# One product of the maxima moved ahead of the two scores in TensorE's order

## What is computed

```python
q = rope(h @ w_down_q.T @ w_up_q.T)          # 16 heads of 64
k = rope(h @ w_down_kv.T @ w_up_k.T)
v = h @ w_down_kv.T @ w_up_v.T
scores = einsum('bhqd,bhkd->bhqk', q, k) / 8
attn = softmax(scores, axis=-1)
out = einsum('bhqk,bhkd->bhqd', attn, v) @ w_out.T + residual
```

## Time and profile before

| | |
|---|---|
| runs: median, lowest, highest | 4357.19, 4356.98, 4368.64 us |
| profiled execution: own time | 4368.48 us |
| profiled execution: span, mean granted TensorE clock | 4366.7 us, 0.967 |
| TensorE matmul busy | 4005.4 us, 92% |
| GpSimd busy | 3049.4 us, 70% |
| ScalarE busy | 3010.3 us, 69% |
| VectorE busy | 2756.6 us, 63% |
| first and last S | start at 613.2 and 3799.9 us of the span |

### The profile page before, as it was taken

How to read it: one execution, slowest core, us unless ns; L and a number is a source line. 1 busy time by engine, 2 the same in 40 slices (tenths; PEclk the granted TensorE clock), 3 DMA queues, 4 the chain that set the end, 5 groups by cost and what they waited for, 6 DMA issues and landing times. The chain is left out here.

```text
span 4366.7 us, 65862 instructions
## 1 busy us (share of the span) xinstructions
PE 4005.4 (92%) x24896; PEld 2256.7 (52%) x24896; DVE 2756.6 (63%) x3555; ACT 3010.3 (69%) x3800; POOL 3049.4 (70%) x1597
## 2 busy tenths in 40 slices
PE   7999869999899989999998999899889999879999
PEld 6888724444344434444444444344444444358888
DVE  5556457656766675766667666766776667345653
ACT  4454348787778777877887787788777887735444
POOL 3444438878778787878887788788877887724444
PEclk9999979999999999999999999999999999979999
DMA  3333221111111211121112112111211121123332
GB/s 109 100 117 107 79 77 52 50 57 61 62 57 54 69 50 57 55 78 53 50 60 69 52 62 69 49 50 59 71 52 59 50 79 52 41 92 117 117 100 66
DMA packets 193645, 301.12 MB, mean 69 GB/s; under 512 B 50766, under 2 KB 101680, under 8 KB 192688
## 3 DMA queue, kind: packets, MB, share of 16 engines
q1 hardware_dynamic: 193328, 296.92, 21.2%
HBM read 201.92 MB, written 26.74 MB: 52 GB/s over the span
## 5 line engine op out<-in xcount | busy, mean ns | idle before, releaser
L988 DVE TENSOR_REDUCE atNM<-atPS 128x2 f32<-128x1024 f32 x1024 | 1205.9, 1220 | 804.0 <-PE atPS L806 801.4
L1053 POOL TENSOR_TENSOR atACC<-atACC,atPT 128x1024 f32<-128x1024 f32 x512 | 1285.1, 2510 | 63.0 <-ACT atPT L922 10.3
L922 ACT ACTIVATE atPT<-atPS 128x1024 f32<-128x1024 f32 x1024 | 995.7, 1023 | 201.7 <-PE atPS L827 195.1
L913 ACT ACTIVATE atPS<-atSH 128x1024 f32<-128x1024 f32 x1024 | 1009.5, 1022 | 87.1 <-DVE atNM L988 45.0
L838 PE MATMUL atPO<-atPT,atV 128*64 128x512 f32 x4096 | 974.3, 596 | 0.0
L1053 POOL TENSOR_TENSOR atACC<-atPT 128x1024 f32<-128x1024 f32 x256 | 624.0, 2437 | 105.3 <-PE atOT L849 103.7
L1032 POOL TENSOR_TENSOR atVT<-atVT,atSIN 128x512 f32<-128x512 f32 x256 | 342.8, 1339 | 366.6 <-DMA atVT<-atR 366.5
L806 PE MATMUL atPS<-atKH,atQH 64*128 64x512 f32 x2048 | 465.1, 455 | 121.0 <-ACT atPT L922 95.1
L838 PEld LDWEIGHTS atPO<-atPT,atV 128*64 128x64 f32 x4096 | 281.2, 137 | 477.1 <-issue 470.4
L827 PE MATMUL atPS<-atQH,atKL 64*128 64x512 f32 x2048 | 476.9, 462 | 45.2 <-ACT atPS L913 45.2
L827 PE MATMUL atPS<-atQH,atKH 64*128 64x512 f32 x2048 | 413.4, 399 | 0.0
(11 more groups left out here) (238 smaller groups left out, 6593.2 us busy)
## 6 DMA issues: line engine op xcount, KB each, us to landing
atVT<-atR SPq DMA_DIRECT2D x512, 128.0 KB, 2.0
atSH<-atMD SPq DMA_DIRECT2D x128, 512.0 KB, 4.4
f1GB<-f1GD SPq DMA_DIRECT2D x128, 256.0 KB, 6.8
atRSUM<-atRD SPq DMA_DIRECT2D x128, 256.0 KB, 4.0
f2GB<-f2GD SPq DMA_DIRECT2D x128, 256.0 KB, 6.9
x<-X SPq DMA_DIRECT2D x7, 1024.0 KB, 4.8
X<-x SPq DMA_DIRECT2D x7, 1024.0 KB, 5.4
f1XB<-in_x SPq DMA_DIRECT2D x5, 1024.0 KB, 5.3
```

What stands on the lines that cost most here:

```text
L913: act.eng.activation(PS[ring.of[("score", n, t, j)]][:, :, :], SH[t][:, :, :], ACT.Copy).then_inc(filled[j % 2].sem)
L922: act.eng.activation(PT[k % NPT][:, :, :], PS[ring.of[step]][:, :, :], ACT.Exp, scale=SCALE).then_inc(grown.sem)
L988: dve.eng.tensor_reduce(NM[:, q // 4, :, q % 4, t], PS[ring.of[step]][:, :, :], AX.X, ALU.max, negate=True).then_inc(most_out.sem)
L1053: pool.eng.tensor_tensor(total[:, :, :], begun[:, :, :], PT[k % NPT][:, :, :], ALU.add).then_inc(gathered.sem)
```

## The change

On each period's place in `order`, M0 now stands ahead of S0 and S1, and M1 stays behind them. No instruction is added or taken away.

```diff
@@ -671,7 +671,7 @@
-                order += begin.get(g, []) + scores + mosts + early.get(g, []) + fills + attends
+                order += begin.get(g, []) + mosts[:1] + scores + mosts[1:] + early.get(g, []) + fills + attends
```

## The result

The changed kernel takes 4515.8 us (median of four runs, 4505.5 to 4530.6), the kernel before 4362.9 beside it: the ratio is 1.035, with a 95% interval from 1.032 to 1.038. It is slower by some 153 us. 101 were forecast: the time lies inside the stated range, which reached to 4545, but 13 us above the forecast's own bounds of 4413 to 4503.

The account below looks back on a forecast made before the run. The prediction took TensorE, busy 92% of the span, as the bound. Its terms gave +13.5 us per sequence, 7 x 13.5 + 6.5 = 101 in all, so 4458 us against a median of 4357.2; range 4350 to 4545.

Parts of the forecast that it names:

- The mechanism: Turn of the ring: M1 no longer waits for E0 but for X0, so VectorE's lateness at X0 delays TensorE.
- some 250 us: Sign in the table of waits: M's wait for X, replacing its 95 us wait for an exponential.
- periods with VectorE free: 28 periods of a sequence: M1 at 1.82 instead of 2.08 us, -0.26 each, -7.3 us per sequence.
- periods 0 and 1 of the even pairs: In period 1, M0 and the scores behind it wait for the queries' copy: +1.2 us each, +4.8 per sequence.
- period 5 of pairs 1, 5, 7: VectorE is busy until 1.82 us into the period, so M1 comes late: +1.0 each, +3.0 us per sequence.
- period 5 of pairs 0 and 6: A rotation of 2.62 us runs into the period and delays X0: +1.5 each, +3.0 us per sequence.
- three more periods of a sequence: Three periods into which a rotation of up to 2.9 us or `qlow` runs: 1.0 each, +3.0 us per sequence.
- norm pairs 2 and 3, periods 4 to 6: VectorE is behind with the layer norm: +1.4 us for each of five periods, +7.0 per sequence.
- Rival 1: VectorE begins X0 earlier and late rotations no longer reach into the next period: 4322 us, chance 0.13.
- Rival 2: Rotations stay pinned to GpSimd's gathers, some six periods of a sequence lose 0.7 us each: 4492 us, chance 0.16.
- Rival 3: Nothing is absorbed: norm-pair periods pay M1's full delay, 5 us in about four periods: 4556 us, chance 0.10.
- rival 4: It evens out: blocked periods cost half, gains and losses cancel: 4357 us, chance 0.08.

## Why the prediction was right, and what it sized too small

*The mechanism* was right: M1 waits for X0, and with the table of tiles, which keeps TensorE's order and takes that wait away, the periods that were long by a late X0 are gone. The sign of "some 250 us" of M waiting for X came with 245. The size is another matter. The parts of the sum, in us over all eight sequences, and what the two traces show from S0 to S0:

| part | forecast | measured |
|---|---|---|
| periods with VectorE free (206 that are in no other row) | -58 | -54 |
| periods 0 and 1 of the even pairs | +38 | +55 |
| period 5 of pairs 1, 5, 7 | +24 | +23 |
| period 5 of pairs 0 and 6 | +24 | +43 |
| three more periods of a sequence | +24 | +9 |
| period 6 of pairs 1, 5, 7 | none | +22 |
| norm pairs 2 and 3, periods 4 to 6 | +49 | +38 |
| periods 0 and 1 of pair 3 | none | +19 |
| period 7 of pair 1 | none | -14 |
| all others | none | +11 |
| sum | +101 | +152 |

Some parts came out dearer than forecast, by about 90 us together, and others cheaper, by about 40. That the total is no further off than 51 is in part luck.

*Free periods.* The -0.26 us a period is right: 212 at -0.263 came.

*Period 5 of the odd pairs.* +1.0 was forecast, +0.91 is the median.

*Period 1 of the even pairs.* The step was right and the term too small: +1.2 each, 38 us, against 55 in the trace of the change and 46 in the experiment that takes it out. M0 comes 7.6 us after period 0 begins, as worked out. In pair 32 the two periods lose 2.4 even so, and the clock is why. The copy, M0 behind it and the first products of S0:

```profile
2297.12 1.05 ACT L896 ACTIVATE atQH<-atU 128x1024 fp32r<-128x1024 f32 x1
...
2298.32 0.79 PE L806 MATMUL atPS<-atKH,atQH 64*128 64x512 f32 x2 [3.38 <-ACT atQH L896]
2298.88 0.65 PE L827 MATMUL atPS<-atQH,atKL 64*128 64x512 f32 x2
...
2299.31 0.65 PE L827 MATMUL atPS<-atQL,atKH 64*128 64x512 f32 x2
```

TensorE has stood still for 3.38 us, and the products then follow every 0.43 us instead of 0.23. In pair 48 it stands still for as long, the products keep their pace, E0 starts 1.4 us behind the copy as forecast, and the two periods lose 1.25:

```profile
3142.41 0.50 PE L806 MATMUL atPS<-atKH,atQH 64*128 64x512 f32 x2 [3.37 <-ACT atQH L896]
3142.72 0.43 PE L827 MATMUL atPS<-atQH,atKL 64*128 64x512 f32 x2
3142.95 0.42 PE L827 MATMUL atPS<-atQL,atKH 64*128 64x512 f32 x2
...
3143.64 1.94 ACT L922 ACTIVATE atPT<-atPS 128x1024 f32<-128x1024 f32 x2 [1.38 <-PE atPS L827]
```

The windows (span, busy of five engines, granted clock, DMA) of period 1 of pair 32 and of pair 36, which loses 1.5 after a shorter wait of 2.07:

```profile
2298.30:2305.00 6.70, 6.68 (x45) 4.36 (x47) 3.58 (x3) 4.20 (x5) 6.56 (x3) 0.78 0.00 0
...
2517.30:2522.50 5.20, 5.20 (x43) 3.02 (x42) 4.35 (x3) 4.03 (x5) 3.96 (x3) 1.00 0.00 0
```

The granted clock averages 0.78 in the one, part of it at the lower of its two levels, and 1.00 in the other. So it goes in all pairs 0 and 4. In seven of them the clock is 1.00 in the 3 us from M0 on, and they lose 1.2 to 1.6 us, from S0 to S0. In the other nine it is 0.50 to 0.72 there, and they lose 2.4 to 3.8. The kernel before has 1.00 at this place in all of them but the very first. The forecast priced the wait, not what may come to the clock behind it.

*Period 5 of pairs 0 and 6.* +1.5 was forecast, the median is +3.4. The step "a rotation of 2.62 runs into the period" did not come: the rotation now starts ahead of the gather and ends 0.57 into the period. It is the inverse (L997) behind it that falls beside the gather, and takes 2.34 us. X0 begins at 3.07, where 2.3 to 2.7 was forecast. Pair 32:

```profile
2320.57 2.82 POOL L1053 TENSOR_TENSOR atACC<-atPT 128x1024 f32<-128x1024 f32 x1
...
2321.07 2.34 DVE L997 TENSOR_TENSOR atRQ<-atRQ 128x16 f32<-128x16 f32 x1
...
2324.93 0.61 PE L806 MATMUL atPS<-atKH,atQH 64*128 64x512 f32 x2 [2.46 <-DVE atNM L988]
2325.47 1.97 PE L785 MATMUL atOT<-atCQ,atWQ 128*64 128x512 f32 x4
```

The projection takes 1.97 instead of 1.08 behind it: the clock again. In pair 38 it stays at 1.00 behind the same wait, and the period loses 1.8:

```profile
2646.73 0.50 PE L806 MATMUL atPS<-atKH,atQH 64*128 64x512 f32 x2 [2.46 <-DVE atNM L988]
2647.17 1.08 PE L785 MATMUL atOT<-atCQ,atWQ 128*64 128x512 f32 x4
```

Four periods with such a wait keep the clock and lose 1.8 each; ten have 0.50 to 0.75 in the 3 us behind M1 and lose 3.4 to 3.7. In the two places together the lower clock is worth some 28 us (an estimate: ten times 1.65, and eight times 1.4 in the pairs 0 and 4), over half of the 51 by which the sum is short.

*Period 6 of the odd pairs.* It was counted among the free ones, or at nothing; it loses 1.1 (median), 22 us. The work of period 5 ends later on VectorE, the rotation behind it meets a gather and runs on into period 6. Pair 39, whose period 6 begins at 2700.84:

```profile
2700.28 2.50 DVE L978 TENSOR_TENSOR atU<-atU,atVT 128x512 f32<-128x512 f32 x1
...
2702.70 1.21 DVE L988 TENSOR_REDUCE atNM<-atPS 128x2 f32<-128x1024 f32 x1
...
2703.97 0.50 PE L806 MATMUL atPS<-atKH,atQH 64*128 64x512 f32 x2 [1.24 <-DVE atNM L988]
```

*The three periods.* The prediction does not name them. In the trace before, VectorE is late by a rotation or `qlow` in period 6 of pair 4 and in periods 0 and 2 of pair 7 (busy until 2.35, 2.34 and 2.05 us into the period), if these are meant. The first cost 9 us; the other two got shorter.

*The norm pairs.* Periods 4 to 6 of pairs 2 and 3 cost less than forecast, 38 us against 49. Left out of the sum were periods 0 and 1 of pair 3, where the layer norm's statistics (L948) stand on VectorE ahead of X0, and the wait for the transfer in pair 1.

*The rivals.* Rival 1 falls: VectorE begins X0 1.4 us earlier where it is free, and the rotation of pairs 0 and 6 does get out of the way, but another step is late in its place, and in period 5 of pair 37 above the same steps are late still. Rival 2's 4492 us lay nearer to the measured 4516 than the forecast's 4458, though its own case, a rotation held in period 5 of pairs 0 and 6, did not come. Its premise, that the gathers hold VectorE, belonged in the sum: with the gathers cut, 130 of the 153 us go. The rule of the Trainium skill on VectorE and GpSimd ("SBUF — State Buffer", "Who interferes with whom") agrees with these runs: rotations of 0.68 without the long gathers, and with them ends 0.54 and 0.55 behind a gather. Rival 3 was too dear, as the norm pairs show, and rival 4 too cheap.

What stays open is why the clock falls behind some of these waits and not behind others of the same length, and how the cost of the norm pairs divides between waits and clock; no run here holds the clock while the waits change.

## What to carry to other kernels

A wait is moved by an order that turns a ring: look up which reader each user of a tile then waits for, and when that reader's engine is free to begin, period by period, not on the average. A step that is moved ahead takes its other waits along, here the copy of the queries, and holds up what now stands behind it. Here a wait for one engine was better covered with other work of the waiting engine (0.990 of the time before) than exchanged for a wait on a third (1.035). And before the cost of a stretch is read from where it begins and ends, look whether a wait has only crossed its border.

## What had not been expected

The gathers on GpSimd cost the kernel before some 105 us (4366 to 4262 us with narrow ones) although GpSimd is busy for only 70% of the span: they stretch VectorE's rotations, inverses and norms, an inverse of 128x16 from 0.17 to 2.34 us. And a wait of TensorE of 2.5 to 3.4 us was in many places, not in all, followed by products at about half their pace, 0.43 us each instead of 0.23, for some 2 us.
